# An order of its own on every engine for the first two turns of a 16-sequence transformer kernel

## The reference

```
x = x + x @ W0[subject].T + b0[subject]
x = x + zX * lap_x(x) + zY * lap_y(x) + zR * x * (1 - x)
x = x + attention(x, side, seq_len)        # 16 heads of 16; keys: x (masked) and the query's own row
x = x + w0 * chosen_expert(x) + w1 * shared_expert_0(x) + w2 * shared_expert_1(x)
```

## Time and profile before

| | |
|---|---|
| median of the runs | 1038.63 us |
| lowest, highest | 1036.63, 1041.29 us |
| profiled execution, own time | 1041.99 us |
| its span | 1040.2 us |
| PE, DVE, ACT, POOL busy | 973.5, 777.6, 688.5, 612.6 us |
| mean granted TensorE clock | 0.963 of full speed |

### The profile page before, as it was taken

How to read it: one execution, slowest core, us unless ns; L and a number is a source line. 1 busy time by engine, 2 the same in 40 slices (tenths; PEclk the granted TensorE clock), 3 DMA queues, 4 the chain that set the end, 5 groups by cost and what they waited for, 6 DMA issues and landing times.

```text
span 1040.2 us, 27614 instructions
## 1 busy us (share of the span) xinstructions
PE 973.5 (94%) x9488; PEld 918.0 (88%) x9488; DVE 777.6 (75%) x1552; ACT 688.5 (66%) x1435; POOL 612.6 (59%) x548
## 2 busy tenths in 40 slices
PE   4669999999999999999999999999999999999896
PEld 4358999999999999999999999999999999999796
DVE  6556688777878877787877878787787878778633
ACT  4465876768587675858667685866768586676641
POOL 6674657567465656647465664756566475656440
PEclk8658999999999999999999999999999999999988
DMA  5626142341524244152424315142532514251110
GB/s 156 178 72 123 49 67 81 81 102 41 102 81 61 81 84 98 41 111 72 61 81 91 92 47 115 62 61 82 98 85 55 115 53 71 72 100 53 42 51 11
DMA packets 91387, 82.68 MB, mean 79 GB/s; under 512 B 11972, under 2 KB 90852, under 8 KB 91364
## 3 DMA queue, kind: packets, MB, share of 16 engines
q1 hardware_dynamic: 91364, 82.38, 34.8%
HBM read 52.59 MB, written 4.20 MB: 55 GB/s over the span
## 4 chain that ended last, share of the span: by engine, by line
PE 56%; issue 12%; ACT 8%; DVE 8%; POOL 6%; SPq 5%; DMA 3%; ACTq 0%; DVEq 0%; POOLq 0%
PE out L553 5%; PE out L555 5%; PE out L554 5%; PE front L668 5%; PE hid L553 4%; PE front L553 4%; PE hid L554 4%; PE hid L555 4%; PE front L555 4%; PE front L554 4%; PE front L655 3%; DMA raw<-in_wo 3%; ACT prob_hi L877 3%; PE pv L610 2%; PE pv L611 2%
## 5 line engine op out<-in xcount | busy, mean ns | idle before, releaser
L1273 POOL TENSOR_TENSOR prob_lo<-prob,prob_hi 128x512 f16<-128x512 f32 x144 | 174.1, 1209 | 121.5 <-ACT prob_hi L877 121.5
L553 PE MATMUL hid<-x_hi,exp_hi 128*128 128x256 f32 x768 | 231.2, 301 | 1.5 <-DVE x_lo L1118 1.5
L553 PE MATMUL out<-hid_hi,exp_hi 128*128 128x256 f32 x768 | 226.5, 295 | 1.9
L554 PE MATMUL hid<-x_lo,exp_hi 128*128 128x256 f32 x768 | 217.1, 283 | 0.0
L555 PE MATMUL hid<-x_hi,exp_lo 128*128 128x256 f32 x768 | 216.3, 282 | 0.0
L554 PE MATMUL out<-hid_lo,exp_hi 128*128 128x256 f32 x768 | 214.3, 279 | 0.0
L555 PE MATMUL out<-hid_hi,exp_lo 128*128 128x256 f32 x768 | 214.1, 279 | 0.0
L1216 POOL TENSOR_TENSOR exp_lo<-raw,exp_hi 128x512 fp32r<-128x512 f32 x128 | 169.7, 1340 | 69.7 <-ACT exp_hi L894 69.6
L1038 DVE TENSOR_REDUCE s_max<-front 128x2 f32<-128x512 f32 x256 | 169.1, 687 | 52.1 <-PE front L655 50.1
L873 ACT ACTIVATE prob<-front 128x512 f32<-128x512 f32 x256 | 153.2, 599 | 51.8 <-PE front L668 51.7
L916 ACT ACTIVATE hid_hi<-hid 128x512 fp32r<-128x512 f32 x192 | 114.6, 597 | 107.0 <-PE hid L555 105.2
(11 more groups left out here) (166 smaller groups left out, 2255.3 us busy)
## 6 DMA issues: line engine op xcount, KB each, us to landing
raw<-in_wi SPq DMA_DIRECT2D x64, 256.0 KB, 3.8
raw<-in_wo SPq DMA_DIRECT2D x64, 256.0 KB, 2.8
q_rows<-w_raw SPq DMA_DIRECT2D x80, 128.0 KB, 3.6
k_rows<-x1T SPq DMA_DIRECT2D x48, 128.0 KB, 4.4
...
```

The source lines that it names most:

```text
L553: nc.tensor.matmul(acc, w_hi, a_hi, start=first, stop=False)
L554: nc.tensor.matmul(acc, w_hi, a_lo, start=False, stop=False)
L1273: nc.gpsimd.tensor_tensor(prob_lo[:, h % NPROB, :], prob[:, h % NPROB, :], prob_hi[:, h % NPROB, :], ALU.subtract).then_inc(prob_split_poo ...
```

## The change

Turns 0 and 1 get five lists of their own (`OPEN_PE`, `OPEN_ACT`, `OPEN_DVE`, `OPEN_POOL`, `OPEN_SP`), in which every stage names its sequence. From turn 2 on the order is the old one. The diff, cut:

```
+OPEN_PE = list(opening("""
+warm x1 bias_q lap q bias_k kp ks vs vp self
+S0 S1 S2 S3 S4 S5 S6 S7 S8 m0 S9 S10 S11 S12 S13 S14 S15 E0 E1 m1 x1.1 E2 E3 E4 E5 E6 q.1 E7 lap.1 E8 E9 E10 E11 kp.1 E12 E13 E14 E15
+pvend vs.1 aT ks.1 wo vp.1 self.1
+"""))
+OPEN_ACT = list(opening("""
+x_parts s_parts w_parts lin0 x1_parts react lin1 lin2 x2_parts q qa lin3 shared0 kp qb kq ks shared1 vs vp x2b
+w_parts.1 x_parts.1 s_parts.1 m0 shared2 E0 E1 m1 shared3 E2 x1_parts.1 react.1 E3 E4 E5 E6 q.1 E7 qa.1 E8 x2_parts.1 E9 E10 E11 kp.1
+E12 E13 E14 E15 qb.1 kq.1 shared4 aT vs.1 ks.1 shared5 x3_parts vp.1 x2b.1 shared6 shared7
+"""))
+OPEN_DVE = list(opening("""
+memsets x_lo s_lo w_lo laps x_parts x1 lin0 x1_parts bias_q react lap x2_parts setup bias_k kp shared0 k3 vp self shared1
+S0 S1 S2 S3 S4 S5 S6 S7 S8 S9 S10 S11 S12 x_parts.1 S13 S14 S15 x1.1 E1 x1_parts.1 react.1 E3 E5 lap.1 E7 x2_parts.1 half E11 kp.1
+E13 E15 att k3.1 aT wo x3_parts vp.1 self.1
+"""))
+OPEN_POOL = list(opening("""
+memsets x1 lin1 lin2 qa lin3 qb ks vp w_parts.1 x_parts.1 s_parts.1 shared2 E0 x1.1 E2 shared3 E4 E6 m1 E8 E9 qa.1 E10 E12 norm E14
+qb.1 shared4 ks.1 shared5 vp.1 shared6 shared7
+"""))
+OPEN_SP = list(opening("""
+mask q0 k0 q1 k1 mask_row q2 k2 load.1 shared2 shared3 shared4 shared5 m0 m1 wi_load E15 kp.1 k3.1 shared6 shared7 gates
+"""))
+STAGES = ["e_out", "gate1", "raw0", "raw1", "e_out", "gate1", "e_out", "gate1"]
+SHARED_DVE = 2
+SHARED_POOL = SHARED - SHARED_DVE
...
+WARM = 16
+            def warm():
+                pe.wait_ge(q_rows_set, 1)
+                for _ in range(WARM):
+                    nc.tensor.matmul(front_bank[0][:, 0:S], q_rows[0:ROWS_MAX, 0, 0:P], q_rows[0:ROWS_MAX, 1, :], start=True, stop=True)
...
                 if s == 0:
                     wait(pe, x3_split, 1, j, 1)
-                    pe.wait_ge(w_split, SHARED)
-                    pe.wait_ge(gate_in, 32)
+                    pe.wait_ge(shared_split_dve, SHARED_DVE)
+                    pe.wait_ge(w_split, 4 - SHARED_DVE)
+                elif s == STEPS:
+                    pe.wait_ge(w_split, SHARED_POOL)
...
+                elif name == "shared6":
+                    sp.wait_ge(w_split, 3)
+                    load_shared(6)
+                elif name == "shared7":
+                    sp.wait_ge(w_split, 4)
+                    load_shared(7)
+                elif name == "gates":
+                    sp.wait_ge(w_split, SHARED_POOL)
```

More of the change, by code:

```diff
@@ L67 @@
 """.split()
-ACT_FIRST = "x_parts w_parts s_parts x1_parts react q qa x2_parts qb kp kq vs ks vp x2b".split()
 DVE_BODY = """
@@ L104, with opening @@
 EARLY = ("x_parts", "x1", "react", "lap")
-SHARED_AT = ["qb", "qb", "vp", "vp", "m0", "m0", "m1", "E8"]
-SHARED = len(SHARED_AT)
-SP_FIRST = "load wo0 wo1 wo2 m0 wo3 E0 E2 E4 E6 m1 wi_load E15 kp k3 vp sum".split()
-assert [x for x in SP_FIRST if x in SP_BODY] == SP_BODY
-LIN_ORDER = [0, 1, 2, 3]
+def opening(text):
+    for word in text.split():
+        name, _, seq = word.partition(".")
+        yield name, int(seq or 0)
+OPEN_PE = list(opening("""
[20 more added lines that the diff above has]
+"""))
+OPEN_RING = [x for x in OPEN_PE if family(x[0])[0]]
+assert len(OPEN_RING) % 2 == 0 and sorted(OPEN_RING) == sorted((x, n) for x in RING for n in range(2 - lag(x)))
+assert [x for x, _ in OPEN_RING[-4:]] == RING[-4:]
+STAGES = ["e_out", "gate1", "raw0", "raw1", "e_out", "gate1", "e_out", "gate1"]
+SHARED = len(STAGES)
+SHARED_DVE = 2
+SHARED_POOL = SHARED - SHARED_DVE
 PARTS = 2 * STEPS
 FIRST, LAST = 2, B
-assert sorted(ACT_FIRST) == sorted(x for x in ACT_BODY if lag(x) == 0)
 def in_turn(i, names):
@@ L138, with in_place @@
 LINKS = {"early": 3, "attention": 4 + 5 + len(HI_DVE), "rest": 8}
+def in_place(name, i):
+    orders = {0: ("x_parts", "s_parts", "w_parts"), 1: ("w_parts", "x_parts", "s_parts")}
+    order = orders[i] if isinstance(i, int) and i in orders else ("x_parts", "w_parts", "s_parts")
+    return order.index(name) + 1
 def wait(eng, sem, per_turn, turn, n):
@@ L344, in build, with front_psum @@
         rest_link = sem("rest_link")
-        def front_psum(name):
+        def front_psum(name, i):
+            if isinstance(i, int) and (name, i) in OPEN_RING:
+                return front_bank[OPEN_RING.index((name, i)) % 2]
             return front_bank[RING.index(name) % 2]
@@ L444, in stage @@
                 if name == "load":
-                    if isinstance(i, int) and i == 0:
-                        return
                     who = chooser(subject_sb, i, w0.shape[0])
@@ L477, in stage @@
                 elif name == "wi_load":
+                    if isinstance(i, int) and i == 0:
+                        sp.wait_ge(choice_in, 32)
                     kind = chooser(label_sb, i, wi.shape[0])
-                    wait(sp, w_split, PARTS, i, SHARED)
+                    wait(sp, w_split, PARTS, i, 4 - SHARED_DVE if isinstance(i, int) and i == 0 else SHARED_POOL)
                     load_wi(kind)
@@ L584, in open_bank @@
             def open_bank(i, name):
+                if isinstance(i, int) and (name, i) in OPEN_RING:
+                    at = OPEN_RING.index((name, i))
+                    if at >= 2:
+                        wait_freed(pe, OPEN_RING[at - 2][1], OPEN_RING[at - 2][0])
+                    return front_psum(name, i)
                 u, turn = RING.index(name), i + lag(name)
@@ L878, in front, with lin_hi_part @@
                     last.then_inc(freed["E"], 1)
-            def lin_hi_parts(first, end):
-                for n in LIN_ORDER[first:end]:
-                    act.wait_ge(lin_in[n], 16)
-                    nc.scalar.activation(lin_hi[:, n, :], raw[:, n * C * D:(n + 1) * C * D], ACT.Copy).then_inc(lin_hi_done, 1)
+            def lin_hi_part(n):
+                act.wait_ge(lin_in[n], 16)
+                nc.scalar.activation(lin_hi[:, n, :], raw[:, n * C * D:(n + 1) * C * D], ACT.Copy).then_inc(lin_hi_done, 1)
             def shared_hi_part(n):
```

303 lines of the change are left out of this document (174 added, 129 removed).

## The result

The changed kernel takes 1044.78 us (median of 4 runs, 1043.37 to 1046.01), the kernel before 1038.18 in the same comparison: a ratio of 1.0059, 95% interval 1.0033 to 1.0086 (formed over all the runs; the two medians alone give 1.0064). It is **slower by some 6 us**; the prediction was 1036.2 with a range up to 1040.0, so it failed in sign as well as in size.

What follows compares the result with a forecast made beforehand. PE was taken to set the pace from turn 2 on, with waste in the opening; -1.4 - 6.6 + 3.6 + 2.0 = -2.4 us gave 1039.6 profiled, 1036.2 us as median, range 1029.5 to 1040.

Steps and rivals of the forecast that it cites:

- Up to S0: Opening until `S0`: gapless row DMAs from 17.7 bring `S0` from 32.44 to 31.0, -1.4 us; bounds 29.0 and 32.4.
- the 12 row DMAs now come without a gap: Turn 0: the row DMAs are a throughput load, 0.97 us each from 17.7, so the rows are there at 30.8.
- DVE slowed beside POOL: Turn 0: 0.3 us counted from a residue of 0.96 instead of 0.69; the harsher shared-port rule meant 1.0 less gain.
- S0 to E15: Opening's middle stretch: pieces 4 to 7 leave the exponentials' path, 41.5 us instead of 48.1, -6.6 us; bounds -9 and -3.
- a bound for that piece: `S0` to `E15`: gain only 3 us if POOL's piece 3, ahead of an exponential's residue, holds ACT back.
- E15 to the attention: End of the opening: distance from `E15` to the attention's end kept, putting that end at 77.9.
- fixed distance: Attention's end to turn 2's first hidden product: stays 6.1 us, so that product starts at 84.0.
- The stall at P0: Turn 2's head: `P0` waits for late pieces 6 and 7, 91.2 instead of 87.6, +3.6 us; bounds +1 and +6.
- two chains: Piece 7's landing: at 88.8 behind sequence 1's row DMAs, or 88.3 behind POOL's piece 5; said to agree within 0.5 us.
- The clock fall: Behind the wait at `P0`: PE's clock falls to half and loses half of some 4 us, +2.0; bounds 0 and +2.5.
- The rival for slower: Turn 2: PE stays cold; at 20 us cold the sum is +5.6, 1044.2 us; chance of slower than 1043: 0.05.
- it does not do what it says: Rival, `S0` to `E15`: exponentials keep their old pace, `E15` gains 3 us, not 8; sum +2.6; chance 0.10.

Runs made afterwards that it cites:

- run 6: Changed kernel with turn 0's query product ahead of the Laplacian, and first query parts ahead of mask and key parts; ratio to the kernel before 1.0062.
- run 4: Changed kernel with one DMA issue moved: the subject's number goes ahead of the first input, as before; ratio to the kernel before 1.0052.
- run 9: Changed kernel with one DVE instruction moved: piece 0's residue goes behind the last key part in turn 0; ratio to the kernel before 1.0056.
- run 11: Changed kernel with the edits of run 4, run 6 and run 9, plus all query rows first in turn 0; ratio to the kernel before 1.0064.
- run 12: Run 11 plus a fifth edit: mask made on DVE ahead of `react` and sent ahead of all rows; ratio to the kernel before 1.0017.
- run 16: Changed kernel with run 12's five edits of turn 0 and run 14's places of pieces 2 to 7; 1031.92 against 1035.57 us for the kernel before.
- run 1: Changed kernel with pieces 2 to 7 of the shared weights at early places; 1039.36 against 1039.18 us for the kernel before.
- run 3: Changed kernel with turn 1 in the order and with the pieces of the kernel before; 1045.31 against 1039.18 us for the kernel before.
- run 8: Changed kernel with only pieces 2 to 5 early, pieces 6 and 7 left at the end; ratio to the kernel before 1.0050.
- run 13: Changed kernel with the turn 0 edits of run 4, run 6 and run 9, and run 14's piece places; 1035.63 against 1036.46 us before.
- run 14: Run 5 with piece 6 on ACT ahead of `q.1` and piece 7 on POOL behind `ks.1`'s keys; 1032.13 against 1036.46 us for the kernel before.
- run 15: Run 14 with POOL's residue of piece 6 placed sooner among the exponentials; 1033.23 against 1037.30 us for the kernel before.
- run 5: Changed kernel with run 2's old turn 0 and run 1's early pieces 2 to 7; 1035.98 against 1037.05 us for the kernel before.
- run 2: Changed kernel with turn 0 in the order, loads and engine division of the kernel before; 1041.62 against 1039.18 us for the kernel before.

## Why the prediction was wrong

By its own steps, in the order of the sum. In the profile turn 3 started at 159.28 where the sum gave 149.6: 9.7 us to explain.

- **Up to S0, predicted -1.4, was +2.55: the step that failed worst, 4.0 us.** The first row DMA at 17.7 came at 20.05, which is 2.3 of it; the first row landed 3.3 us behind its issue where the sum had 2.4, and the twelve landed 1.03 us apart instead of 0.97, together 1.6. So the load went nearly as reckoned from a start that was wrong; but "the 12 row DMAs now come without a gap" was not so for their issue, and once the start was mended alone (run 6), the gaps bound. I did not walk each group of the new list to the instruction that makes it. Things I had in the diff held them: SP's wait for the subject's number behind `x` (1.5 alone, run 4), piece 0 on DVE ahead of the last key part (1.1, run 9), the query product behind the Laplacian (0.8, run 6, within the scatter), and behind these the second query group behind `kp` on ACT and the mask issued late (together with them 31.57, runs 11 and 12). The single gains don't add: each uncovers the next.
- **DVE slowed beside POOL, 0.3 us.** It cost 0.65 in `x_lo` (1.34) and 0.90 in `react` (1.65) alone. I had weighed the row of 0.96 against a rule and kept the row. `react` started 0.7 us into POOL's first half of `lin1` (14.49, 1.8 long) and ended 0.6 us behind that half; in runs 12 and 16, with POOL idle beside it, it took 0.75. The Trainium skill, page "SBUF — State Buffer", in its account of the shared port pair, says that whoever starts first holds the pair for its whole instruction. The trace agrees with that for `react`, and the 1.0 it would have taken from the gain was the better price for these instructions. How much of it reached `S0` no run separates.
- **S0 to E15, predicted -6.6, was -4.04: right in mechanism, 2.5 too much.** `S15` is read 14.7 us behind `S0` (predicted 14.5). Then most of the miss arises between `x1.1` and `q.1`: `x1.1` ends 19.7 us behind `S0` (the walk had 19.1), `q.1` starts 26.9 behind it (24.9), `kp.1` ends 38.9 behind it (36.2). There PE waits 1.60 at 58.41 and 1.28 at 61.51, the second for the first of the two DVE residues above, 1.63 us long beside POOL's piece 3. The walk had a bound for that piece, but the piece is not the reason: in run 1, where it stands ahead of `E0`, PE waits 1.15 and 1.17 at the same places and `q.1` starts 26.8 behind `S0`, because POOL's residues of the exponentials then run beside DVE's (1.53). So, as far as the second wait shows, the term left out is DVE slowed beside POOL, whatever POOL does; no run took that overlap away, and the first wait stays open. Run 3 shows from the other side that the new order gains 7.1 us for the same `S0`.
- **E15 to the attention, taken as unchanged, was +1.24.** Piece 4 on POOL (82.36 to 84.93) makes DVE's product with `v_self` 1.95 instead of 0.62. Runs 8 and 13 to 16, with no piece there, take 5.10 to 5.31; all with a piece there 6.5 to 6.7.
- **The attention to the first hidden product, taken as "fixed distance" 6.1, was 7.71: 1.6 too little.** See below: the clock.
- **The stall at P0, predicted +3.6, was +3.48: right,** with its two chains, ACT waiting on the DMA for both pieces, and the DVE's `hid_lo` as releaser. Its size is partly luck: `P0` came 14.75 us behind the attention where the sum had 13.3, and the wait kept its size because the first hidden product was as late (run 8, with a gap of 6.57, waits 4.41). The two chains were not within 0.5 us of each other either, but 1.7. Runs 1, 5 and 13 to 16 take the wait away; run 8 shows that taking away POOL's chain alone is not enough.
- **The clock fall, predicted +2.0, was +2.46: right.** From `P0` to turn 3 the eight profiles without the stall take 56.30 to 56.48 us, the ten with it 57.82 to 59.17. Of the ten, runs 2, 4 and 8 have the full clock back 3.2 to 3.6 us behind `P0` and take 57.82 to 58.01; the other seven have it back 5.4 to 6.1 behind and take 58.79 to 59.17.

The last two are 5.9 us, with the 1.6 of the gap 7.5; the -8.0 that should have paid for them was -0.25 at the attention's end, which leaves the 7.3 by which turn 3 starts later. The rival for slower (PE cold for 20 us of turn 2) did not come about: the clock was low for 6 to 7 us. The costs of the stall were on the list; what was missing was a rival in which the opening gives nothing. The nearest, "it does not do what it says", let `E15` gain 3 us by an old pace of the exponentials; it gained 1.5, with the pace improved and `S0` late.
